# The order of one unit of row maxima within a cycle of an attention loop: first excess ahead of the scores, first base behind the second score tile, second base behind the fourth

## What is computed

```python
x = x + attention(layernorm(x))
# attention, per head:
scores = (Q @ K.T) * scale            # 2048 x 2048
scores = where(mask, scores, -inf)    # block L1: causal; block L3: a mask by regions, plus a bias row
attn = softmax(scores, axis=-1)
out_h = attn @ V
out = concat(out_h) @ W_O + b_O
```

## Time and profile before

| what | before |
|---|---|
| median of 3 runs | 3845.22 us (3842.68 to 3849.38) |
| the profiled execution's own time | 3847.62 us |
| its span in the profile | 3845.9 us |
| TensorE matmuls busy | 3630.9 us (94% of the span) |
| VectorE busy | 2835.3 us (74%) |
| ScalarE busy | 2268.7 us (59%) |
| GpSimd busy | 423.9 us (11%) |
| mean granted TensorE clock | 0.976 |

### The profile page before, as it was taken

One profiled execution on the slowest core, in us unless ns is written; L12 is line 12 of the kernel. 1 busy time (PEld: TensorE's weight loads), 2 busy tenths in 40 slices (PEclk: granted clock), 3 DMA queues, 4 the chain that ended last, 5 costly groups with the idle time before them and its releaser, 6 DMA issues.

```text
span 3845.9 us, 65564 instructions
## 1 busy us (share of the span) xinstructions
PE 3630.9 (94%) x24697; PEld 1904.7 (50%) x24697; DVE 2835.3 (74%) x5691; ACT 2268.7 (59%) x2644; POOL 423.9 (11%) x486
## 2 busy tenths in 40 slices
PE   5999999999999978999999997799999999999999
PEld 3545454454545434555555555255545455554545
DVE  6777878777777776777777776477777777777775
ACT  4666666666666515566566653566666666666664
POOL 2000000000000002232322221000000000000000
PEclk9999999999999988999999997899999999999999
DMA  1000000000000000000000000000000000000000
GB/s 48 8 9 10 10 12 8 9 10 10 7 10 7 15 5 7 12 15 15 13 15 11 13 13 3 22 5 12 8 9 10 10 9 11 9 7 11 7 10 15
DMA packets 43632, 43.08 MB, mean 11 GB/s; under 512 B 16210, under 2 KB 30298, under 8 KB 43066
## 3 DMA queue, kind: packets, MB, share of 16 engines
q1 hardware_dynamic: 43322, 38.88, 3.4%
HBM read 36.38 MB, written 1.69 MB: 10 GB/s over the span
## 4 chain that ended last, share of the span: by engine, by line
PE 85%; DVE 8%; ACT 3%; issue 2%; SPq 1%; DMA 1%; POOL 0%; DVEq 0%; ACTq 0%
PE ps L592 81%; DVE wexp L1365 2%; DVE over L1365 1%; DVE acc L1343 1%; DVE x L1537 1%; ACT work L1070 1%; PE ps L925 1%; PE ps L936 1%; SPq L499 0%; ACT Kh L1040 0%; DMA auxQ<-mrow 0%; PE ps L965 0%; PE ps L864 0%; DVE V L1274 0%; DVE stats L1262 0%
## 5 line engine op out<-in xcount | busy, mean ns | idle before, releaser
L1070 ACT ACTIVATE work<-ps 128x1024 f32<-128x1024 f32 (+1 forms) x1344 | 1275.4, 995 | 927.3 <-PE ps L592 921.4
L1343 DVE TENSOR_TENSOR acc<-acc,work 128x1024 f32<-128x1024 f32 (+2 forms) x1152 | 1361.5, 1182 | 58.9 <-ACT work L1070 14.3
L592 PE MATMUL ps<-work,V 128*64 128x512 f32 (+3 forms) x5376 | 1234.1, 579 | 0.0
L592 PEld LDWEIGHTS ps<-work,V 128*64 128x64 f32 x5376 | 449.4, 137 | 542.7 <-issue 448.4
L592 PE MATMUL ps<-Qh,Kh 64*128 64x512 f32 (+3 forms) x2688 | 658.4, 485 | 32.9 <-issue 10.7
L1365 DVE CUSTOM_DVE_ANT_0 over<-ps,over,mpart 128x512 f32<-128x512 f32 (+3 forms) x642 | 422.8, 696 | 351.0 <-PE ps L592 350.9
L592 PE MATMUL ps<-Qh,Kl 64*128 64x512 f32 (+3 forms) x2688 | 525.7, 386 | 0.0
L592 PE MATMUL ps<-Ql,Kh 64*128 64x512 f32 (+3 forms) x2688 | 522.4, 383 | 0.0
L592 PE MATMUL ps<-auxQ,auxK 64*128 64x512 bf16 (+3 forms) x2688 | 518.5, 380 | 0.0
L1365 DVE CUSTOM_DVE_ANT_0 wexp<-ps,wexp 128x512 f32<-128x512 f32 (+1 forms) x632 | 376.8, 636 | 25.7 <-PE ps L592 20.4
L592 PE MATMUL ps<-Kh,Qh 64*128 64x512 f32 (+2 forms) x1520 | 344.0, 465 | 16.5 <-DVE mpart L1365 7.4
(11 more groups left out here) (190 smaller groups left out, 2681.2 us busy)
## 6 DMA issues: line engine op xcount, KB each, us to landing
rden<-inverse_sums SPq DMA_DIRECT2D x186, 128.0 KB, 2.9
auxQ<-mrow SPq DMA_DIRECT2D x384, 1.0 KB
wqk<-in_wqk SPq DMA_DIRECT2D x24, 128.0 KB, 2.5
dcomp<-rden SPq DMA_DIRECT2D x186, 2.0 KB
wv<-in_wv SPq DMA_DIRECT2D x24, 64.0 KB, 2.3
inverse_sums<-rcomp SPq DMA_DIRECT2D x93, 4.0 KB, 1.3
work<-in_mlp_w SPq DMA_DIRECT2D x1, 1024.0 KB
work<-in_c_aux SPq DMA_DIRECT2D x1, 1024.0 KB, 4.8
```

Of the source, the lines that this page charges most:

```text
L592: return pe.matmul(o, w, m, start=start, stop=stop, skip_group_check=True)
L1070: act.activation(work[:, 2 * e:2 * e + 2, q0:CH], ps[:, b:b + 2, q0:CH], ACT.Exp, scale=L.scale).then_inc(s["p_ready"], 1)
L1343: dve.tensor_tensor(o, o, work[:, slots[two]:slots[two] + 2, q0:CH], ALU.add).then_inc(s["acc_ready"], 1)
```

## The change

Both units of cycle x are now begun and ended in cycle x:
- TensorE: excess 0 stands at the start of the row block, ahead of the first score tile, and waits for the tops of the last unit. Base 0 stands behind the second score tile, and waits for Relu 0. Base 1 stands behind the fourth score tile and waits for tops 0; excess 1 follows it, as before once tile 2's exponentials are done. Where there is a `tile0`, it takes base 1's place, and base 1 comes behind excess 1.
- ScalarE: Relu 0 ahead of the four exponentials, Relu 1 right behind them, then the jobs.
- GpSimd (layer 1): the cut of unit 0 ahead of everything in the cycle, that of unit 1 behind the cuts of the exponentials.
- VectorE: the last addition of the cycle before, tops 0, the inverse, addition 0, (the `mt` job), (tile 0's reduction), addition 1, tops 1, (the other slot-0 job), addition 2, jobs 1 and 2. `tops` now waits itself for the Relu, and the base matmuls no longer do in general.

The numbers of instructions stay the same on every engine.

```diff
@@ class Layer
     def tile0_in(self, x):
-        found = [m for sl, m, u in self.units_in(x - 1) if self.featured and u == 1]
+        found = [m for sl, m, u in self.units_in(x) if self.featured and u == 1]
@@ TensorE
                 def base(h, p, u, b0=MAXB):
-                    pe.wait_ge(s["relu_ready"], L.NR * h + L.relus_to[u] + 1)
                     for _, t, col, b, nb, _, ends in L.units[u]:
@@ row_block
-                    pending = {sl: (m, u) for sl, m, u in L.units_in(x - 1)}
+                    units = {sl: (m, u) for sl, m, u in L.units_in(x)}
                     c = L.steps[2 * g][0]
-                    if 0 in pending:
-                        m, u = pending[0]
-                        base(m, m % 2, u)
+                    if 0 in units:
+                        m, u = units[0]
+                        at_least(pe, s["top_ready"], L.NTOP * m + L.tops_to[u])
+                        excess(m, m % 2, u, MAXB)
...
-                    if 1 in pending:
-                        m, u = pending[1]
-                        pe.wait_ge(s["relu_ready"], L.NR * m + L.relus_to[u] + 1)
+                    for sl, m, u in L.units_in(x - 1):
+                        if sl:
+                            pe.wait_ge(s["relu_ready"], L.NR * m + L.relus_to[u] + 1)
                     scores(n, p, 2 * g, 0)
...
                     scores(n, p, 2 * g, 1)
-                    m0 = L.tile0_in(x)
-                    if m0 is not None:
-                        pe.wait_ge(s["bias_in"], 64 * m0 + 64)
-                        tile0(m0, m0 % 2)
-                        pe.wait_ge(s["p_ready"], tiles + 1)
-                        scores(n, p, 2 * g + 1, 0)
-                    if 1 in pending:
-                        m, u = pending[1]
-                        at_least(pe, s["top_ready"], L.NTOP * m + L.tops_to[u])
+                    if 0 in units:
+                        m, u = units[0]
+                        pe.wait_ge(s["relu_ready"], L.NR * m + L.relus_to[u] + 1)
                         base(m, m % 2, u)
-                    if m0 is None:
-                        pe.wait_ge(s["p_ready"], tiles + 1)
-                        scores(n, p, 2 * g + 1, 0)
+                    pe.wait_ge(s["p_ready"], tiles + 1)
+                    scores(n, p, 2 * g + 1, 0)
                     pe.wait_ge(s["p_ready"], tiles + 2)
                     scores(n, p, 2 * g + 1, 1)
-                    units = L.units_in(x)
-                    for sl, m, u in units:
-                        if sl:
-                            pe.wait_ge(s["p_ready"], tiles + 3)
-                        at_least(pe, s["top_ready"], L.NTOP * units[0][1] + L.tops_to[units[0][2]])
-                        excess(m, m % 2, u, SCA if sl else MAXB)
+                    if 1 in units:
+                        m, u = units[1]
+                        m0 = L.tile0_in(x)
+                        if m0 is not None:
+                            pe.wait_ge(s["bias_in"], 64 * m0 + 64)
+                            tile0(m0, m0 % 2)
+                        else:
+                            at_least(pe, s["top_ready"], L.NTOP * m + L.tops_to[u])
+                            base(m, m % 2, u)
+                        pe.wait_ge(s["p_ready"], tiles + 3)
+                        excess(m, m % 2, u, SCA)
+                        if m0 is not None:
+                            pe.wait_ge(s["top_ready"], L.NTOP * m + L.tops_to[u])
+                            base(m, m % 2, u)
@@ ScalarE, cycle: clip(slot) is the Relu of that slot's unit
+                    clip(0)
                     if L.main(x):
...
-                    for slot in range(2):
...
-                        jobs(slot)
+                    clip(1)
+                    jobs(0)
+                    jobs(1)
@@ GpSimd, cycle
+                    units = L.units_in(x)
+                    for sl, m, u in units:
+                        if sl == 0:
+                            cut_unit(m, u, sl)
                     for m, c in L.due(L.mul_at, x):
                         normalise(m, c)
...
-                    for sl, m, u in L.units_in(x):
-                        cut_unit(m, u, sl)
+                    for sl, m, u in units:
+                        if sl:
+                            cut_unit(m, u, sl)
@@ VectorE, tops
+                    dve.wait_ge(s["relu_ready"], L.NR * h + L.relus_to[u] + 1)
                     dve.wait_ge(s["mb_ready"], based)
@@ VectorE, cycle
-                    before_ = L.units_in(x - 1)
+                    units = L.units_in(x)
...
+                    rows_of_maxima = any(sl == 0 and kind == "mt" for sl, kind, _, _ in L.jobs_in(x))
+                    for which in last:
+                        add(*which)
+                    for sl, m, u in units:
                         if sl == 0:
                             tops(m, u)
-                    for which in last:
-                        add(*which)
-                    if L.tile0_in(x) is not None:
-                        tops(L.tile0_in(x), 0)
-                    for sl, m, u in before_:
-                        if sl == 1:
-                            tops(m, u, slot=1)
                     for m, c in L.due(L.inv_at, x):
                         inverse(m, c)
                     for which in sums[:1]:
                         add(*which)
-                    jobs(0)
-                    for which in sums[1:-1]:
+                    if rows_of_maxima:
+                        jobs(0)
+                    if L.tile0_in(x) is not None:
+                        tops(L.tile0_in(x), 0)
+                    for which in sums[1:2]:
+                        add(*which)
+                    for sl, m, u in units:
+                        if sl == 1:
+                            tops(m, u, slot=1)
+                    if not rows_of_maxima:
+                        jobs(0)
+                    for which in sums[2:-1]:
                         add(*which)
```

More of the change, by code:

```diff
@@ L782, in opening @@
                         if kind == "mt" and based is not None:
+                            pe.wait_ge(s["relu_ready"], L.relus_to[based[0]] + 1)
                             base(0, 0, *based)
@@ L1058, in cycle, with clip @@
                         deviations(NEXT_LN[L.n], c)
+                    def clip(slot):
+                        for sl, m, u in L.units_in(x):
+                            if sl == slot:
+                                w = L.units[u][-1][2] + L.units[u][-1][4] * P
+                                b = SCA if sl else MAXB
+                                act.wait_ge(s["md_ready"], L.NR * m + L.relus_to[u] + 1)
+                                act.activation(excess_of(sl)[:, :, 0:w], ps[:, b:b + 2, 0:w], ACT.Relu)\
+                                    .then_inc(s["relu_ready"], 1)
+                    clip(0)
                     if L.main(x):
@@ L1071, in cycle @@
                                            scale=L.scale).then_inc(s["p_ready"], 1)
-                    for slot in range(2):
-                        for sl, m, u in L.units_in(x):
-                            if sl == slot:
-                                w = L.units[u][-1][2] + L.units[u][-1][4] * P
-                                b = SCA if sl else MAXB
-                                act.wait_ge(s["md_ready"], L.NR * m + L.relus_to[u] + 1)
-                                act.activation(excess_of(sl)[:, :, 0:w], ps[:, b:b + 2, 0:w], ACT.Relu)\
-                                    .then_inc(s["relu_ready"], 1)
-                        jobs(slot)
+                    clip(1)
+                    jobs(0)
+                    jobs(1)
                     for m, c in L.due(L.out_at, x):
```

1 line of the change is left out of this document (removed).

## The result

The changed kernel takes 3821.23 us (median of 4 runs, 3817.99 to 3822.36) against 3846.57 us for the one before beside it: a ratio of 0.9934, 95% interval 0.992 to 0.9948. That is 25.3 us less, 0.66%. The forecast was 3825 us. The profiled execution has a span of 3820.6 us.

The account below looks back on a forecast made before the run. TensorE, busy 94% of the span, was taken as the bound, with layer 1 holding most of its gap. Terms -11 -11 -7 -6 +4 +5 +4 +2 sum to -20 us, giving 3825 us; range 3804 to 3852 us.

Parts of the forecast that it names:

- What bounds the kernel: Whole kernel: TensorE busy 94% of the span, gain only from its idle time, layer 1's gap of 47.8 us the largest.
- The full cycle stays as it is: Layer 0's full cycle stays at 9.73 us; Relu 0 just fits before exponential 0, with 0.03 us to spare.
- g = 9 and g = 2: Diagonal cycles of layer 1: TensorE's wait for tops 1 before an excess goes, 1.4 us times 8 pairs, -11 us each.
- g = 0 and g = 5: Diagonal cycles of layer 1: about half of the remaining `mpart` and `mcol` waits go, -7 us.
- g = 4: Full cycle of layer 1: base 1 leaves the gap too short for its tops, 0.7 us per pair, -6 us.
- Relu 0 behind a copy of Q or K: Layer 1 cycles with such a copy on ScalarE: exponential 0 comes 0.14 to 0.2 us later, +4 us.
- g = 6: Layer 1 cycle with a short column block: tops 1 end late, near 9.6 us, up to 0.9 us times 8; +5 us taken.
- The cut of unit 0: Layer 1, new on the path from Relu 0 to tops 0: +4 us, bounds 0 and +20 us.
- the rival: Layer 1: unit 0's cuts, stretched behind VectorE's last addition, delay tops 0 and base 1; +20 us, 3843 us, chance 0.15.
- Layers 0 and 2: Their loops: `mpart` waits go, -8 us, against delays of +3, +4 and +3 us; together +2 us.
- Several signs: Right: layer 1 `mpart` waits under 12 us, g = 9 near 5.1 us, TensorE busy unchanged; wrong: new waits on exponentials.
- the third rival: Small waits hidden in modelled busy time go too, layer 1's gap closes almost wholly: -45 us, 3800 us, chance 0.12.

Follow-up runs that it names:

- the runs by layer: New order in layer 1 alone: 3823.26 us, ratio 0.9941 to the kernel before; in layers 0 and 2 alone: 3843.25 us, ratio 0.9992.

## Why the prediction was right

Point by point, by its own steps:

- **What bounds the kernel.** TensorE, and the gain is in layer 1: right, and shown by the runs by layer. That it would come out of TensorE's idle time was right in part: layer 1's gap gives 7.3 us of 19.7.
- **The full cycle stays as it is.** Right, nearly to the number: exponential 0 was put at 1.47 and 0.05 later behind a copy, tops 0 at 2.8 to 4.15; measured 1.51 and 2.78 to 4.13. Layer 0's loop changes by +1.0 us.
- **g = 9 and g = 2**, -11 us each: too much. They get 1.10 and 1.02 us shorter by the medians, not 1.4. The waits before an excess went as I said. Base 1's wait for tops 0 is 0.44 us in the usual g = 9, close to the 0.5 that I put; what was off is when it ends. Tops 0 run from 3.2 to about 4.6 us and not from 3.0 to 4.35, so base 1 starts at 4.68 and the column block at 5.34, not 5.05. The sums over all pairs, -8.8 and -12.5 us, have 6.1 us of the clock in them, for which I had no term.
- **g = 0 and g = 5**, -7 us: -0.48 and -0.68 us by the medians; summed -3.5, since the loop's first cycle is 4.85 us longer.
- **g = 4**, -6 us: -6.1. I left g = 7 out, and it gives -3.8.
- **Relu 0 behind a copy of Q or K**, +4 us: this term failed. The cycles in which a copy stands first on ScalarE are g = 2, 4, 6 and 9; at g = 2 and 9 exponential 0 starts 0.08 to 0.09 us later than before, and at g = 6 it starts 0.26 us later, but the column block, at 5.73 against 5.70 us, does not follow. What gets longer is g = 1, 3 and 8, by 5.0 us in all, and there no copy precedes the Relu. At g = 1 and 8 the excess in front of the scores is wider than the base that stood there, so the scores start 0.12 and 0.17 us later and the column block 0.17 and 0.16 us later. At g = 3 the row block is as long as before, and the cycle ends at 8.68 us, right behind tops 1 (8.62). A like number from other causes: luck.
- **g = 6**, +5 us: the mechanism was right and the size was not, 1.43 us by the median and +10.0 in all, above my own bound of 0.9 us times 8. Tops 1 end at 10.45 us and not near 9.6. About 0.5 us of this is the long cut (9.92 without any cut); the rest goes with addition 1 ahead of tops 1 (9.46 with the two exchanged).
- **The cut of unit 0**, +4 us with bounds 0 and 20: some 3 us. At g = 2 and 9 it is as the rival had it: the cut takes 1.20 us and ends at 2.98 and 3.00. The Trainium skill's lock (SBUF — State Buffer, same section) is seen in these rows. But in six of the ten cycles the cut is short, and where it is long base 0 lands hardly earlier: tops 0 would start only 0.07 us sooner at g = 2 and 9.
- **Layers 0 and 2**, +2 us: -1.2 us in the loops, and 3.1 us less in the run, within noise of nothing. The cycles behind a chunk's end are 0.05 us longer, as forecast; g = 15 is not longer at all, since tops 1 end there at 8.96 us and not at 9.1.

Layer 1's terms added up to -22 us, and its loop gave -19.7. This agreement is in part luck. I multiplied by 8 what only the six middle pairs gain, and I had no term for the clock. Without the clock's 6.1 us the loop gained some 14 us, and the clock filled most of what was missing. A total gain of 20 was forecast and 25 measured, and the remaining 4 us lie outside the loops, where I had forecast nothing. The direction, the layer and the largest cycles are right by their mechanism; the closeness of the sum is not to be credited to it.

Several signs that the prediction named came out against it. The `mpart` waits of layer 1 fell to 18.4 us and not under 12, and 13.8 of these stand before an excess, 9.3 of them at the end of g = 6; this was also on the list of what would show it wrong. So were waits on the exponentials that were not there: they came, 6.8 us in 29, in the diagonal cycles. g = 9 takes 5.34 us to its column block, not 5.1. And TensorE's busy sum, said to stay, fell from 3630.9 to 3613.8 us. Of the third rival (waits hidden in modelled busy time go too) the cause was thus at work, and its -45 us were not reached.

## What to carry to other kernels

When a chain goes round several engines, write down the distances between its steps on the bound engine and put each step into a gap that is longer than the answer takes; here the short gap before the excess moved out and the long values block moved in. Then look at what is in front of each answer in its own engine's queue: the same new order on TensorE is 0.66% faster or 1.8% slower, depending on one addition on VectorE. And where an instruction of GpSimd lies on the path, ask which VectorE instruction will be running as it starts. Last, a gain per steady cycle is not to be multiplied by all repeats: here the first and the last of eight head pairs gained nothing or next to it.

## What the runs showed of the hardware

- A cut of 128x256 on GpSimd takes 0.41 us while VectorE is idle or in a tops, and up to 1.41 us with an addition of two SBUF inputs begun just before it. Over the 44 cuts of unit 1 in layer 1's window: with tops 1 put ahead of addition 1, the maximum falls from 1.41 to 0.45 us. All 131 cuts of layer 1 that begin within an addition end 0.26 to 0.28 us after it, so how long one takes follows from how much of the addition is left.
- A Relu of 128x32 in front of another reads as 0.19 us long but moves the next one by 0.07 us, the distance of starts.
- TensorE's granted clock can fall to its level of 1.2 GHz in the middle of a loop. In layer 1 before, 4 of 15 waits of 1.15 to 1.38 us at g = 2 and 9 were followed by such a stretch (granted clock 0.57 over 1936 to 1940 us, behind the wait of the earlier trace rows). Each cost 1.4 to 1.6 us: that head pair's g = 2 took 14.26 us where the median is 12.68. In the changed kernel none of the seven waits of 1.33 us at the end of g = 6 is followed by one. Whether shorter waits keep the clock up was not tried by itself.
